# Mixer phase: scans that begin at zero, the old state added to the first column, a third state added by VectorE in four blocks

## The chip, the cores and the metric

One core of one Trainium2 chip runs the whole kernel in one launch. The metric is the time of that core in microseconds (us). Before the change the median of three runs is 5242.94 us (5242.02 to 5242.97). About 0.2% (10 us) is what such a measurement can tell from no change.

## The reference

The input is a tensor of 4 sequences x 2048 tokens x 512 channels in float32. Three layers follow one another: an RWKV-like channel mix (`f1`), a Mamba mixer, and the channel mix again (`f2`). The change is in the mixer alone:

```
h   = layernorm(x); x_in = h - mean(h)
xz  = x_in @ W_in                        # 512 -> 2 x 1024: u's input and the gate z
u   = silu(conv4(xz_first) + conv_b)
B,C = split(u @ W_x)                     # 16 states each
delta = softplus(u @ W_dt + b_dt)
for t:  h = exp(delta_t * A) * h + delta_t * B_t * u_t      # 1024 channels x 16 states
        y_t = sum over states of h * C_t
out = (y + u * D) * silu(z) @ W_out + residual
```

## The kernel before

The mixer goes through the tokens in 32 chunks of T = 256, 8 chunks (MC) to a sequence. In a chunk the 1024 channels are 8 blocks b of 128 partitions, and the 16 states of a block are 4 groups g of SG = 4 states. A (block, group) pair is a unit n = 4b + g, so a chunk has NU = 32 units; g is called the place of a unit in its block below. Each engine has its own instruction list with one slot for each unit, written out by hand. Tables such as `DU_AT`, `DT_AT` and `YG_AT` say in which slot a piece of other work (the convolution, the projections, softplus) stands, and `due(...)` finds what falls into a slot. Semaphores order the engines.

For a unit:

- ScalarE (L1153) writes exp(delta * A) for 4 states into PSUM, two states (`SD`) to a bank, three banks in turn. The half of a unit that goes to bank p may be written when bank p - 3 has been used: for the second half of unit n that is when VectorE's product `times_c` (L1253) of unit n - 1 has been done. `keep_psum` (L1094) and `keep` (L1076) copy the last column of every scan to `hst`, the state carried to the next chunk.
- GpSimd (POOL) makes `mx_dbu` = B * (delta * u) (`times_b`, L947) for two units in one instruction, 128 x 2048 elements, into one of two pairs of buffers; it starts only when the unit three before its first has been scanned. It also makes delta * u (`delta_u`, L964), adds the softplus parts (`add_log`, L935) and multiplies the two SBUF states of a unit by C (`times_c`, L960, mostly two units in one instruction). All of these read and write SBUF.
- VectorE (DVE) runs the four scans of 256 steps (L1241). Each reads the decay from PSUM, dbu from SBUF, and as its initial value a column of `hst` (zero in a sequence's first chunk). Two scans write back to PSUM and are multiplied by C by L1253, two write to `hp` in SBUF.
- TensorE (PE) sums the 16 products of a block into `ps_y` by multiplying with an identity matrix. The last SBUF state of the units at places 2 and 3 is left out there, and VectorE adds it (`add_state`, L1220) before the product with the gate (`gated`, L1227).

At place 0 VectorE also does three convolution taps (L1210). At place 1 it does the two adds and the gated product of the block before last. After the slot of place 1 in every second (odd) block ScalarE switches its function table, does two silu instructions, and switches back (L1182 to L1187).

Of VectorE's instructions in the mixer before the change, none has two tensor inputs in SBUF: scans, L1253, L1210, L1220 and L1227 all read one of their two tensors from PSUM. The channel-mix phases have such instructions, for example L511, L482 and L445.

Of the kernel before, what the change touches and what calls it, by code (L numbers as in the profile page):

```python
# [19 lines left out]
P = 128  # L20
# [667 lines left out]
def mixer_phase(nc, hT_pad, xs_in, ahead, w_dt, w_out, w_k, mu_r, mu_k, bc_dram, out):  # L688
# [8 lines left out]
    with ExitStack() as ctx:  # L697
# [20 lines left out]
        cs = sb("cs", [P, NG, SG, T])  # L718
        bc = sb("bc", [2 * DS, T])
        dbu = sb("dbu", [P, NM, SG, T])  # L720
# [56 lines left out]
        IN_AT = [NG * b - NU - 9 for b in range(ND)]  # L777
        GATE_AT = [NG * b - 11 for b in range(ND)]
        BC_AT, CLEAR = [-10], -1
        DU_AT = [NG * b - 1 for b in range(ND)]  # L780
        DT_AT = [NG * b - 8 for b in range(ND)]
        U_SILU_AT = [2 * NG * k - NU - 3 for k in range(ND // 2)]
        Z_SILU_AT = [2 * NG * k - 3 for k in range(ND // 2)]
        SKIP_AT = [NG * b + NG - 1 for b in range(ND)]
        YG_AT = [NG * b + NG + 5 for b in range(ND)]
        OUT_AT = [NU - 6, NU - 2, NU + 2, NU + 7, NU + 11, NU + 14, NU + 15, NU + 18]
# [38 lines left out]
        def over_chunks(eng, prologue, body, epilogue=None):  # L825

            if prologue:
                prologue()
            for c in range(MC):
                body(c, c % 2, c == 0)  # L830
            with eng.Fori(1, BATCH - 1) as b:
                for c in range(MC):
                    body(MC * b + c, c % 2, c == 0)
            for c in range(MC):
                body(MC * (BATCH - 1) + c, c % 2, c == 0)
            if epilogue:
                epilogue()

        @block.sync
        def _(sp):  # L840
# [8 lines left out]

            def store_bc(i):  # L850

                sp.wait_ge(s_bc, 16 * (i + 1))
                sp.dma_start(bc_dram[:, :], bc[:, :]).then_inc(s_bcd, 16)

# [5 lines left out]
            def chunk(i, par, b_next, c_next):  # L860

                sp.wait_ge(s_pz, ND * (i + 1))
                if not (isinstance(i, int) and i + 2 > LAST):
                    load_hT(b_next, c_next, par)
                if not is0(i):
                    store_out(i - 1)
                    sp.wait_ge(s_out, 16 * i)
                    sp.dma_start(xo[:, :, :], xs_v[i]).then_inc(s_x, 16)
                store_bc(i + 1)
# [15 lines left out]
            sp.dma_start(xo[:, :, :], xs_v[0]).then_inc(s_x, 16)  # L885
            store_bc(0)
            sp.wait_ge(s_bcd, 16)
# [37 lines left out]
        def _(pool):  # L925
# [46 lines left out]

            def body(i, par, first):
# [20 lines left out]
        def _(act):  # L994
# [54 lines left out]

            def copy_bc(c):  # L1050
                act.wait_ge(s_pb, c + 1)
                if not is0(c):
                    act.wait_ge(s_bcd, 16 * c)
                A.activation(bc[:, :], ps_c[0:2 * DS, 0:T], ACT.Copy).then_inc(s_bc, 16)

# [46 lines left out]
            def prologue():  # L1102
                act.wait_ge(s_wv, 16 * 6)
                A.preload_act_table_set("silu_and_others")
                for n in range(EARLIEST, 0):
                    for b, c in due_before(BC_AT, n + 1, COPY):
                        copy_bc(c)
                    for b, c in due_before(IN_AT, n, TAPS):
# [28 lines left out]

            def body(i, par, first):
                for n in range(NU):
# [30 lines left out]
                    for bb, s in due(BC_AT, n, i, COPY):  # L1170
                        copy_bc(i + s)
                    for j, s in due(EVAC_AT, n, i):
# [24 lines left out]
        def _(dve):  # L1197
# [5 lines left out]
            def conv(c, cp, b, step):  # L1203
# [4 lines left out]
                else:  # L1208
                    dve.wait_ge(s_cv, (KC - 2) * ND * c + ((KC - 2) * b + step - 1))
                V.scalar_tensor_tensor(out=q, in0=in_bank(b)[:, step:step + T], scalar=cw[:, step, b:b + 1],  # L1210
                                       in1=q, op0=ALU.mult, op1=ALU.add).then_inc(s_cq if step == KC - 1 else s_cv, 1)

            def add_state(c, b, k):

# [3 lines left out]
                else:  # L1218
                    dve.wait_ge(s_ya, 2 * (ND * c + b) + k)
                V.tensor_tensor(y, y, hp[:, (NG * (b + 1) - 2 + k) % NH, SG - SD - 1, :], ALU.add).then_inc(s_ya, 1)  # L1220

            def gated(c, cp, b):

                q = gy[:, cp, b, :]
                dve.wait_ge(s_zs, ND * c + (b + 1))
                dve.wait_ge(s_ya, 2 * (ND * c + b) + 2)
                V.tensor_tensor(q, y_sum(b), q, ALU.mult).then_inc(s_g, 1)  # L1227
# [5 lines left out]

            def scan(i, n, half, k, first):
                b, g = divmod(n, NG)
                p = 2 * n + half
                if k == 0:
# [18 lines left out]
            def prologue():  # L1256
                weights()
                for n in range(EARLIEST, 0):
                    for b, c in due_before(IN_AT, n, TAPS):
                        for step in range(1, KC):  # L1260
                            conv(c, c, b, step)

            def add_due(i, n, k):

                for b, s in due(YG_AT, n, i):
                    add_state(i + s, b, k)

# [9 lines left out]

            def body(i, par, first):
                for n in range(NU):
                    if not first:  # L1280
                        dve.wait_ge(s_st, NU * i + (n + 1 - NU))
                        if n == 0:
                            dve.wait_ge(s_kd, NU * i - 2)
                        if n == NU - 2:
                            dve.wait_ge(s_kd, NU * i)
# [3 lines left out]
                    scan(i, n, 0, 0, first)  # L1289
                    scan(i, n, 0, 1, first)  # L1290
                    add_due(i, n, 0)
                    scan(i, n, 1, 0, first)
                    taps(i, par, n, 1)
                    times_c(i, n)
                    add_due(i, n, 1)
                    taps(i, par, n, 2)
                    scan(i, n, 1, 1, first)
                    finish(i, par, n)
                    taps(i, par, n, 3)

            def epilogue():
                for n in range(NU):
                    for b in due_after(YG_AT, n):
                        add_state(LAST, b, 0)
                        add_state(LAST, b, 1)
                        gated(LAST, LAST % 2, b)
# [6 lines left out]
        def _(pe):  # L1313
# [228 lines left out]
```

## Time and profile before

| | us |
|---|---|
| median of three runs | 5242.94 |
| the profiled execution itself | 5241.57 |
| its span (first to last instruction) | 5239.8 |
| first to last scan | 709 to 4622 |
| busy: PE / DVE / ACT / POOL | 5133.1 / 4689.6 / 3829.7 / 4029.3 |
| granted TensorE clock, mean | 0.995 of full |

Busy time counts the stretches in which an engine has an instruction under way. Durations of successive instructions on one engine overlap by some tens of ns, so the distance from start to start, called the pitch here, is what a row of instructions costs. The mixer is about 3913 us of the span; its 32 chunks repeat nearly exactly.

### The profile page before, as it was taken

To read this page: it belongs to the slowest core of one execution; us is meant where nothing else is said; L and a number is where in the kernel's file an instruction comes from. 1 tells how busy PE (TensorE), PEld (TensorE's weight loads), DVE (VectorE), ACT (ScalarE), POOL (GpSimd) and SP (SyncE) were. 2 spreads that over 40 slices of the span, in tenths; PEclk is the share of its full clock that TensorE was granted. 3 is DMA by queue.
4 is the path that set the end of the run, shared out by engine and by line. 5 is a ranking of instruction groups with operands and counts; after the bars stand their busy time and mean duration, and the time that the engine had idled before them with its cause. 6 is when DMAs were issued, how large, how long until landed. Compare 5 with 4: busy or idle time off the path is not lost. (4 is left out here: it accounts for less than half of the span.)

```text
span 5239.8 us, 76968 instructions
## 1 busy us (share of the span) xinstructions
PE 5133.1 (98%) x22400; PEld 4127.8 (79%) x22400; DVE 4689.6 (89%) x8052; ACT 3829.7 (73%) x9592; POOL 4029.3 (77%) x1701
## 2 busy tenths in 40 slices
PE   8999989999999999999999999999999999989999
PEld 6777767888888887878888888888888888768887
DVE  7777679999999999999999999999999999977775
ACT  5566568888888888888888888888888888744443
POOL 1111069999999999999999999999999999941110
PEclk9999999999999999999999999999999999989999
DMA  2322231111111111111111111111111111111111
GB/s 83 97 73 86 95 109 45 46 45 53 57 53 49 45 45 46 45 45 45 50 53 47 46 51 56 53 54 45 45 45 45 45 45 45 65 53 57 65 57 41
DMA packets 137371, 291.74 MB, mean 56 GB/s; under 512 B 23280, under 2 KB 40688, under 8 KB 136944
## 3 DMA queue, kind: packets, MB, share of 16 engines
q1 hardware_dynamic: 136944, 286.75, 16.6%
q8 instruction: 183, 3.00, 0.2%
q14 instruction: 244, 2.00, 0.1%
HBM read 218.53 MB, written 68.18 MB: 55 GB/s over the span
## 5 line engine op out<-in xcount | busy, mean ns | idle before, releaser
L947 POOL TENSOR_TENSOR mx_dbu<-mx_bs,mx_du 128x2048 f32<-128x2048 f32 (+1 forms) x513 | 2321.6, 4526 | 64.1 <-POOL mx_du L964 30.5
L1153 ACT ACTIVATE mx_ps_da<-mx_dl,mx_a 128x256 f32<-128x256 f32 x4096 | 1775.9, 465 | 53.8 <-DVE mx_hp L1241 19.0
L1241 DVE TENSOR_TENSOR_SCAN mx_hp<-mx_ps_da,mx_hst,mx_dbu 128x256 f32<-128x256 f32 x1792 | 1317.5, 735 | 31.2 <-ACT mx_ps_da L1153 31.1
L1241 DVE TENSOR_TENSOR_SCAN mx_ps_da<-mx_ps_da,mx_hst,mx_dbu 128x256 f32<-128x256 f32 x1792 | 1238.8, 736 | 62.9 <-ACT mx_ps_da L1153 56.2
L960 POOL TENSOR_TENSOR mx_hp<-mx_hp,mx_cs 128x1024 f32<-128x1024 f32 (+1 forms) x576 | 1219.6, 2123 | 2.1 <-ACT mx_hst L1076 2.1
L1389 PE MATMUL mx_ps_y<-mx_hc,mx_ident 128*128 128x256 f32 x4096 | 1055.4, 380 | 2.5 <-ACT mx_ps_y L1015 2.5
L1356 PE MATMUL mx_ps_m<-mx_u,mx_w_dt 128*128 128x256 f32 x4096 | 926.0, 379 | 1.7 <-issue 1.7
L1389 PEld LDWEIGHTS mx_ps_y<-mx_hc,mx_ident 128*128 128x128 f32 x4096 | 780.4, 191 | 110.7 <-ACT mx_ps_y L1015 3.5
L1399 PE MATMUL mx_ps_y<-mx_hp,mx_ident 128*128 128x256 f32 x3072 | 841.2, 383 | 23.4 <-POOL mx_hp L960 22.3
L1356 PEld LDWEIGHTS mx_ps_m<-mx_u,mx_w_dt 128*128 128x128 f32 x4096 | 778.1, 190 | 108.2 <-issue 2.5
L1399 PEld LDWEIGHTS mx_ps_y<-mx_hp,mx_ident 128*128 128x128 f32 x3072 | 576.5, 190 | 203.3 <-issue 88.5
L1253 DVE TENSOR_TENSOR mx_hc<-mx_ps_da,mx_cs 128x512 f32<-128x512 f32 x1024 | 684.4, 668 | 1.6 <-PE mx_ps_y L1389 1.6
L1094 ACT ACTIVATE mx_hst<-mx_ps_da 128x2 f32<-128x2 f32 x1022 | 171.0, 167 | 599.2 <-DVE mx_hc L1253 596.6
L246 POOL TENSOR_TENSOR f_rstd<-f_ve,f_half 128x4 f32<-128x4 f32 x48 | 48.4, 1008 | 681.6 <-DVE f_ve L413 681.6
L1338 PE MATMUL mx_ps_m<-mx_hT,mx_w_in 128*128 128x256 f32 x2048 | 493.1, 383 | 19.2 <-DVE mx_u L1210 19.0
L1327 PE MATMUL mx_ps_m<-mx_hT,mx_w_in 128*128 128x259 f32 x2048 | 492.8, 383 | 5.1 <-PEq L59 3.2
L1327 PEld LDWEIGHTS mx_ps_m<-mx_hT,mx_w_in 128*128 128x128 f32 x2048 | 389.9, 191 | 104.9 <-issue 46.4
L1366 PE MATMUL mx_ps_c<-mx_w_out,mx_gy 128*128 128x512 f32 x992 | 466.1, 592 | 0.0
L1338 PEld LDWEIGHTS mx_ps_m<-mx_hT,mx_w_in 128*128 128x128 f32 x2048 | 382.3, 190 | 93.8 <-DVE mx_u L1210 42.6
L1210 DVE SCALAR_TENSOR_TENSOR mx_u<-mx_ps_m,mx_cw,mx_u 128x256 f32<-128x256 f32 x768 | 356.4, 464 | 28.6 <-ACT mx_u L1002 27.8
L252 POOL TENSOR_TENSOR mx_w_in<-f_xhT 128x2048 f32<-128x2048 f32 x30 | 111.1, 3703 | 322.0 <-ACT f_xhT L302 322.0
L1366 PEld LDWEIGHTS mx_ps_c<-mx_w_out,mx_gy 128*128 128x128 f32 x992 | 188.5, 190 | 131.4 <-issue 118.6
(122 smaller groups left out, 7323.7 us busy)
## 6 DMA issues: line engine op xcount, KB each, us to landing
mx_bs<-bc_scratch SPq DMA_DIRECT2D x128, 512.0 KB, 4.4
mx_cs<-bc_scratch SPq DMA_DIRECT2D x128, 512.0 KB, 3.8
mx_hT<-hT_scratch SPq DMA_DIRECT2D x32, 518.0 KB, 4.2
hT_scratch<-f_h2T SPq DMA_DIRECT2D x16, 1024.0 KB, 9.1
mx_xo<-xs_scratch SPq DMA_DIRECT2D x32, 512.0 KB, 3.6
x_scratch<-mx_xo SPq DMA_DIRECT2D x32, 512.0 KB, 2.8
f_x<-in_L_attn_inp SPq DMA_DIRECT2D x12, 1024.0 KB, 6.6
xs_scratch<-f_x SPq DMA_DIRECT2D x12, 1024.0 KB, 4.3
```

Source lines behind the costliest of these rows:

```text
L947: G.tensor_tensor(dbu[:, n % NM:n % NM + k].rearrange("p n s t -> p (n s) t"), bs[:, g:g + k].rearrange("p n s t -> p (n s) t"), bcast(du[ ...
L960: G.tensor_tensor(h, h, cs[:, g:g + k, SD:SG, :], ALU.mult).then_inc(s_pr, k)
L1153: ins = A.activation(ps_da[DA_BANK[p]][:, k, :], dl[:, b % NL, :], ACT.Exp, scale=a_sb[:, b, s:s + 1])
L1210: V.scalar_tensor_tensor(out=q, in0=in_bank(b)[:, step:step + T], scalar=cw[:, step, b:b + 1], in1=q, op0=ALU.mult, op1=ALU.add).then_inc( ...
L1241: ins = V.tensor_tensor_scan(da if half == 0 else hp[:, n % NH, k, :], da, dbu[:, n % NM, s, :], 0.0 if first else hst[:, b, SG * g + s:SG ...
L1253: V.tensor_tensor(hc[:, n % NC, :, :], ps_da[DA_BANK[2 * n]][:, :, :], cs[:, g, 0:SD, :], ALU.mult).then_inc(s_m2, 1)
L1327: ins = M.matmul(in_bank(b)[:, 0:TH], w_in_sb[:, f, b * P:(b + 1) * P], hT[cp][:, f, :], start=(f == 0), stop=(f == NB - 1))
L1338: ins = M.matmul(m_bank(b)[:, 0:T], w_in_sb[:, f, DI + b * P:DI + (b + 1) * P], hT[cp][:, f, PAD_L:PAD_L + T], start=(f == 0), stop=(f == ...
L1356: ins = M.matmul(m_bank(b)[:, 0:T], w_dt_sb[:, k, b * P:(b + 1) * P], u[:, cp, k, :], start=(k == 0), stop=(k == ND - 1))
L1366: ins = M.matmul(ps_c[:, :], gy[:, cp, b, j * P:(j + 1) * P], w_out_sb[:, b, :], start=False, stop=(b == ND - 1), skip_group_check=True)
L1389: ins = M.matmul(y_sum(b), ident[:, :], hc[:, n % NC, k, :], start=False, stop=False, skip_group_check=True)
L1399: ins = M.matmul(y_sum(b), ident[:, :], hp[:, n % NH, k, :], start=False, stop=(g == NG - 1), skip_group_check=True)
```

## The change

All scans start from 0.0. What the initial value did is done ahead of the scan: ScalarE computes the decay of a block's first column for all 16 states (`first_decay`), VectorE multiplies the block's 16 kept states by it (`decay_old`; a memset in the very first chunk), and adds the result to the first column of dbu of two units (`add_old`, 128 x 8 elements), except in a sequence's first chunk. The tile `bc` is dropped; its 32 x 256 values pass through the last block of `gy`. In odd blocks VectorE adds a third state, and PE sums one fewer. `delta_u` moves one slot up, to stand ahead of POOL's product with C and no longer directly ahead of the `times_b` that reads it.

```diff
-        bc = sb("bc", [2 * DS, T])
+        e0 = sb("e0", [P, 2, DS])
...
+        E0_AT = [NG * b - 1 for b in range(ND)]
-        DU_AT = [NG * b - 1 for b in range(ND)]
+        DU_AT = [NG * b - 2 for b in range(ND)]
+        ADDED = [[n for n in range(NG * b + 1 + (b % 2 == 0), NG * (b + 1))] for b in range(ND)]
...
+        def bc(cp):
+            return gy[0:2 * DS, cp, ND - 1, :]
...                                     # POOL, body
+                    for bb, s in due(DU_AT, n, i):
+                        delta_u(i + s, (par + s) % 2, bb)
                     for m, s in due(TIMES_AT, n, i):
                         times_c(i + s, TIMES[m])
-                    for bb, s in due(DU_AT, n, i):
-                        delta_u(i + s, (par + s) % 2, bb)
...                                     # ACT
+                if b == ND - 1:                       # in copy_z
+                    act.wait_ge(s_bcd, 16 * (c + 1))
-                if not is0(c):                        # in copy_bc
-                    act.wait_ge(s_bcd, 16 * c)
+                if not (isinstance(c, int) and c < 2):
+                    act.wait_ge(s_po, TJ * (c - 1))
+            def first_decay(c, b):
+                act.wait_ge(s_dl, ND * c + (b + 1))
+                A.activation(e0[:, b % 2, :], a_sb[:, b, :], ACT.Exp, scale=dl[:, b % NL, 0:1]).then_inc(s_e0, 1)
...                                     # ACT, body, at the end of the slot, after log:
+                    for bb, s in due(E0_AT, n, i):
+                        first_decay(i + s, bb)
...                                     # DVE
-                                           0.0 if first else hst[:, b, SG * g + s:SG * g + s + 1], ALU.mult, ALU.add)
+                                           0.0, ALU.mult, ALU.add)
+            def decay_old(i, b):
+                dve.wait_ge(s_e0, ND * i + (b + 1))
+                h = hst[:, b, :]
+                if is0(i):
+                    V.memset(h, 0.0).then_inc(s_hw, 1)
+                    return
+                dve.wait_ge(s_st, NU * (i - 1) + NG * (b + 1))
+                dve.wait_ge(s_kd, NU * (i - 1) + NG * (b + 1))
+                V.tensor_tensor(h, h, e0[:, b % 2, :], ALU.mult).then_inc(s_hw, 1)
+            def add_old(i, n):
+                b, g = divmod(n, NG)
+                dve.wait_ge(s_hw, ND * i + (b + 1))
+                dve.wait_ge(s_m1, NU * i + (n + 2))
+                d = dbu[:, n % NM:n % NM + 2, :, 0]
+                V.tensor_tensor(d, d, hst[:, b, SG * g:SG * (g + 2)].rearrange("p (n s) -> p n s", n=2),
+                                ALU.add).then_inc(s_hb, 1)
...                                     # DVE, body
-                    if not first:
-                        dve.wait_ge(s_st, NU * i + (n + 1 - NU))
...
+                    if c > 0 and n % 2 == 0:
+                        dve.wait_ge(s_hb, NU // 2 * ((MC - 1) * q + (c - 1)) + (n // 2 + 1))
...
-                    scan(i, n, 0, 1, first)
                     add_due(i, n, 0)
+                    if n % NG == NG - 1 and n < NU - 1:
+                        decay_old(i, n // NG + 1)
+                    elif n == NU - 1 and not (isinstance(i, int) and i == LAST):
+                        decay_old(i + 1, 0)
+                    scan(i, n, 0, 1)
+                    add_due(i, n, 1)
+                    scan(i, n, 1, 0)
                     taps(i, par, n, 1)
                     times_c(i, n)
-                    add_due(i, n, 1)
+                    add_due(i, n, 2)
                     taps(i, par, n, 2)
-                    scan(i, n, 1, 1, first)
+                    if n % 2 and n < NU - 1 and c > 0:
+                        add_old(i, n + 1)
+                    elif n == NU - 1 and c < MC - 1:
+                        add_old(i + 1, 0)
+                    scan(i, n, 1, 1)
...                                     # PE, sum_states
-                last = 1 if g >= NG - 2 else 0
+                last = 1 if n in ADDED[b] else 0
```

## Rows read from the trace of the kernel before

**Rows 1.** Windows: us, then busy us of PE, PEld, DVE, ACT, POOL; clock, DMA.
```profile
1565.00:1687.30 122.30, 121.73 (x529) 98.20 (x528) 119.17 (x209) 99.70 (x270) 120.30 (x50) 1.00 0.15 48
1687.30:1808.80 121.50, 121.09 (x527) 97.91 (x526) 112.58 (x209) 99.11 (x270) 119.65 (x51) 1.00 0.15 49
```
**Rows 2.** All scans by line, until 4622 us: ns min/median/max, first and last start.
```profile
L1241 DVE TENSOR_TENSOR_SCAN mx_ps_da<-mx_ps_da,mx_hst,mx_dbu x1792: 720/733/760, 829.2 to 4620.0; 128x256 f32<-128x256 f32 x200
L1241 DVE TENSOR_TENSOR_SCAN mx_hp<-mx_ps_da,mx_hst,mx_dbu x1792: 711/739/752, 830.5 to 4621.8; 128x256 f32<-128x256 f32 x200
L1241 DVE TENSOR_TENSOR_SCAN mx_ps_da<-mx_ps_da,mx_dbu x256: 669/673/699, 709.3 to 3766.9; 128x256 f32<-128x256 f32 x128
L1241 DVE TENSOR_TENSOR_SCAN mx_hp<-mx_ps_da,mx_dbu x256: 660/679/692, 710.8 to 3768.7; 128x256 f32<-128x256 f32 x128
```
**Rows 3.** Timeline of DVE, first scans of chunks 8 and 9: start us, us.
```profile
1687.29 1.25 DVE L1241 TENSOR_TENSOR_SCAN mx_ps_da<-mx_ps_da,mx_dbu 128x256 f32<-128x256 f32 x2
...
1808.81 1.37 DVE L1241 TENSOR_TENSOR_SCAN mx_ps_da<-mx_ps_da,mx_hst,mx_dbu 128x256 f32<-128x256 f32 x2
```
**Rows 4.** Timeline of DVE, first scans of seven units (places 2, 2, 3, 0, 1, 2, 3).
```profile
2047.50 1.40 DVE L1241 TENSOR_TENSOR_SCAN mx_ps_da<-mx_ps_da,mx_hst,mx_dbu 128x256 f32<-128x256 f32 x2 [0.39 <-ACT mx_ps_da L1153]
...
2062.78 1.39 DVE L1241 TENSOR_TENSOR_SCAN mx_ps_da<-mx_ps_da,mx_hst,mx_dbu 128x256 f32<-128x256 f32 x2
...
2065.96 1.38 DVE L1241 TENSOR_TENSOR_SCAN mx_ps_da<-mx_ps_da,mx_hst,mx_dbu 128x256 f32<-128x256 f32 x2
...
2069.13 1.38 DVE L1241 TENSOR_TENSOR_SCAN mx_ps_da<-mx_ps_da,mx_hst,mx_dbu 128x256 f32<-128x256 f32 x2
...
2073.45 1.39 DVE L1241 TENSOR_TENSOR_SCAN mx_ps_da<-mx_ps_da,mx_hst,mx_dbu 128x256 f32<-128x256 f32 x2
...
2078.08 1.40 DVE L1241 TENSOR_TENSOR_SCAN mx_ps_da<-mx_ps_da,mx_hst,mx_dbu 128x256 f32<-128x256 f32 x2 [0.39 <-ACT mx_ps_da L1153]
...
2081.71 1.37 DVE L1241 TENSOR_TENSOR_SCAN mx_ps_da<-mx_ps_da,mx_hst,mx_dbu 128x256 f32<-128x256 f32 x2
```
**Rows 5.** Timeline of ACT in the same stretch.
```profile
2065.42 0.17 ACT L1094 ACTIVATE mx_hst<-mx_ps_da 128x2 f32<-128x2 f32 x1 [0.88 <-DVE mx_hc L1253]
...
2066.54 0.40 ACT L1070 ACTIVATE mx_en<-mx_en 128x256 f32<-128x256 f32 x1
...
2073.41 1.28 ACT L1182 ACT_TABLE_LOAD   x1
...
2077.17 0.87 ACT L1153 ACTIVATE mx_ps_da<-mx_dl,mx_a 128x256 f32<-128x256 f32 x2
...
2082.66 0.40 ACT L1070 ACTIVATE mx_en<-mx_en 128x256 f32<-128x256 f32 x1
```
**Rows 6.** The page's fifth part, the exponentials' row: count, busy, mean ns of one.
```profile
L1153 ACT ACTIVATE mx_ps_da<-mx_dl,mx_a 128x256 f32<-128x256 f32 x4096 | 1775.9, 465 | 53.8 <-DVE mx_hp L1241 19.0
```
**Rows 7.** Timeline of POOL in the same stretch.
```profile
2062.99 4.52 POOL L947 TENSOR_TENSOR mx_dbu<-mx_bs,mx_du 128x2048 f32<-128x2048 f32 x1 [0.22 <-POOL mx_du L964]
2067.48 2.35 POOL L960 TENSOR_TENSOR mx_hp<-mx_hp,mx_cs 128x1024 f32<-128x1024 f32 x1
2069.79 0.72 POOL L935 TENSOR_TENSOR mx_dl<-mx_dl,mx_en 128x256 f32<-128x256 f32 x1
```
**Rows 8.** Timeline of DVE and of POOL about 113 us, in the first phase.
```profile
113.02 3.69 DVE L511 SCALAR_TENSOR_TENSOR f_x<-f_rt,f_x 128x512 f32<-128x512 f32 x1
...
112.56 3.60 POOL L252 TENSOR_TENSOR mx_w_in<-f_xhT 128x2048 f32<-128x2048 f32 x1 [9.11 <-ACT f_xhT L302]
```
**Rows 9.** Lines 511, 508 and 482: ns min/median/max of the whole run.
```profile
L511 DVE SCALAR_TENSOR_TENSOR f_x<-f_rt,f_x x96: 691/693/4120, 113.0 to 5236.6; 128x512 f32<-128x512 f32 x96
L508 DVE SCALAR_TENSOR_TENSOR f_rt<-f_rt,f_ps_v x128: 669/679/690, 73.1 to 5235.9; 128x512 f32<-128x512 f32 x128
L482 DVE SCALAR_TENSOR_TENSOR mx_w_in<-mx_w_in,f_mu,f_xhT x4: 740/1474/1522, 18.5 to 22.7; 128x512 f32<-128x512 f32 x4
```
**Rows 10.** Groups of DVE: the cheapest small instruction in the trace.
```profile
L409 DVE MEMSET f_mark<- 128x1 f32 x48 | 2.8, 59 | 0.0
```

More of the change, by code:

```diff
@@ L755, in mixer_phase @@
         s_da = sem("da_ready")
+        s_e0 = sem("first_decay_ready")
+        s_hw = sem("old_states_decayed")
+        s_hb = sem("old_states_added")
         s_sc = sem("scanned")
@@ L829, in over_chunks @@
             for c in range(MC):
-                body(c, c % 2, c == 0)
+                body(c, c % 2, 0, c)
             with eng.Fori(1, BATCH - 1) as b:
                 for c in range(MC):
-                    body(MC * b + c, c % 2, c == 0)
+                    body(MC * b + c, c % 2, b, c)
             for c in range(MC):
-                body(MC * (BATCH - 1) + c, c % 2, c == 0)
+                body(MC * (BATCH - 1) + c, c % 2, BATCH - 1, c)
             if epilogue:
@@ L848, in spread, with store_bc @@
                              rows.unsqueeze(0).to_broadcast([P, SG * T])).then_inc(done[g], 16)
-            def store_bc(i):
+            def store_bc(i, par):
                 sp.wait_ge(s_bc, 16 * (i + 1))
-                sp.dma_start(bc_dram[:, :], bc[:, :]).then_inc(s_bcd, 16)
+                sp.dma_start(bc_dram[:, :], bc(par)).then_inc(s_bcd, 16)
             def store_out(i):
@@ L868, in chunk @@
                     sp.dma_start(xo[:, :, :], xs_v[i]).then_inc(s_x, 16)
-                store_bc(i + 1)
+                store_bc(i + 1, 1 - par)
                 sp.wait_ge(s_bcd, 16 * (i + 2))
@@ L885, in _ @@
             sp.dma_start(xo[:, :, :], xs_v[0]).then_inc(s_x, 16)
-            store_bc(0)
+            store_bc(0, 0)
             sp.wait_ge(s_bcd, 16)
@@ L971, in prologue, with body @@
                         delta_u(c, c, b)
-            def body(i, par, first):
+            def body(i, par, q, c):
                 for n in range(NU):
@@ L1048, in clear_bc, with copy_bc @@
                              scale=0.0).then_inc(s_bz, 1)
-            def copy_bc(c):
+            def copy_bc(c, cp):
                 act.wait_ge(s_pb, c + 1)
-                if not is0(c):
-                    act.wait_ge(s_bcd, 16 * c)
-                A.activation(bc[:, :], ps_c[0:2 * DS, 0:T], ACT.Copy).then_inc(s_bc, 16)
+                if not (isinstance(c, int) and c < 2):
+                    act.wait_ge(s_po, TJ * (c - 1))
+                A.activation(bc(cp), ps_c[0:2 * DS, 0:T], ACT.Copy).then_inc(s_bc, 16)
             def relu(c, b):
@@ L1106, in prologue @@
                     for b, c in due_before(BC_AT, n + 1, COPY):
-                        copy_bc(c)
+                        copy_bc(c, c)
                     for b, c in due_before(IN_AT, n, TAPS):
@@ L1128, in prologue @@
                             log(c, b)
+                    for b, c in due_before(E0_AT, n):
+                        first_decay(c, b)
                     if due_before(Z_SILU_AT, n):
@@ L1136, in prologue, with body @@
                         A.preload_act_table_set("natural_log_exp_and_others")
-            def body(i, par, first):
+            def body(i, par, q, c):
                 for n in range(NU):
@@ L1170, in body @@
                     for bb, s in due(BC_AT, n, i, COPY):
-                        copy_bc(i + s)
+                        copy_bc(i + s, (par + s) % 2)
                     for j, s in due(EVAC_AT, n, i):
@@ L1211, in conv, with added_before @@
                                        in1=q, op0=ALU.mult, op1=ALU.add).then_inc(s_cq if step == KC - 1 else s_cv, 1)
+            def added_before(c, b):
+                return sum(len(a) for a in ADDED) * c + sum(len(a) for a in ADDED[:b])
             def add_state(c, b, k):
@@ L1218, in add_state @@
                 else:
-                    dve.wait_ge(s_ya, 2 * (ND * c + b) + k)
-                V.tensor_tensor(y, y, hp[:, (NG * (b + 1) - 2 + k) % NH, SG - SD - 1, :], ALU.add).then_inc(s_ya, 1)
+                    dve.wait_ge(s_ya, added_before(c, b) + k)
+                V.tensor_tensor(y, y, hp[:, ADDED[b][k] % NH, SG - SD - 1, :], ALU.add).then_inc(s_ya, 1)
             def gated(c, cp, b):
@@ L1225, in gated @@
                 dve.wait_ge(s_zs, ND * c + (b + 1))
-                dve.wait_ge(s_ya, 2 * (ND * c + b) + 2)
+                dve.wait_ge(s_ya, added_before(c, b + 1))
                 V.tensor_tensor(q, y_sum(b), q, ALU.mult).then_inc(s_g, 1)
@@ L1232, in last_residual, with scan @@
                 V.tensor_tensor(xo[:, j, :], ps_m[j][:, :], xo[:, j, :], ALU.add).then_inc(s_o, 1)
-            def scan(i, n, half, k, first):
+            def scan(i, n, half, k):
                 b, g = divmod(n, NG)
@@ L1261, in prologue @@
                             conv(c, c, b, step)
+                decay_old(0, 0)
             def add_due(i, n, k):
                 for b, s in due(YG_AT, n, i):
-                    add_state(i + s, b, k)
+                    if k + len(ADDED[b]) >= 3:
+                        add_state(i + s, b, k + len(ADDED[b]) - 3)
             def finish(i, par, n):
@@ L1276, in taps, with body @@
                     conv(i + s, (par + s) % 2, b, step)
-            def body(i, par, first):
+            def body(i, par, q, c):
                 for n in range(NU):
-                    if not first:
-                        dve.wait_ge(s_st, NU * i + (n + 1 - NU))
[L1282 to L1285, printed above, removed]
+                    if c > 0 and n % 2 == 0:
+                        dve.wait_ge(s_hb, NU // 2 * ((MC - 1) * q + (c - 1)) + (n // 2 + 1))
                     dve.wait_ge(s_m1, NU * i + (n + 1))
@@ L1288, in body @@
                         dve.wait_ge(s_r, NU * i + (n - NH + 1))
-                    scan(i, n, 0, 0, first)
-                    scan(i, n, 0, 1, first)
+                    scan(i, n, 0, 0)
                     add_due(i, n, 0)
-                    scan(i, n, 1, 0, first)
+                    if n % NG == NG - 1 and n < NU - 1:
[5 more added lines that the diff above has]
+                    scan(i, n, 1, 0)
                     taps(i, par, n, 1)
                     times_c(i, n)
-                    add_due(i, n, 1)
+                    add_due(i, n, 2)
                     taps(i, par, n, 2)
-                    scan(i, n, 1, 1, first)
+                    if n % 2 and n < NU - 1 and c > 0:
[3 more added lines that the diff above has]
+                    scan(i, n, 1, 1)
                     finish(i, par, n)
@@ L1303, in epilogue @@
                     for b in due_after(YG_AT, n):
-                        add_state(LAST, b, 0)
-                        add_state(LAST, b, 1)
+                        for k in range(len(ADDED[b])):
+                            add_state(LAST, b, k)
                         gated(LAST, LAST % 2, b)
@@ L1419, in prologue, with body @@
                 pe.wait_ge(s_wo, 16)
-            def body(i, par, first):
+            def body(i, par, q, c):
                 for n in range(NU):
```

## The prediction

> **What bounds the kernel now.** I read the windows first [rows 1], because the change is in the mixer only. In an ordinary chunk of 122.3 us PE is busy 121.7, POOL 120.3 and DVE 119.2: three engines within 2%, so busy shares can't name the bound. The reader should instead look at what repeats. The first scan that takes an old state starts at 829.20 [rows 2], the next sequence's first scan at 1687.29 [rows 3]: 7 chunks, 122.58 us each. A sequence's first chunk, whose scans begin at zero already, takes 1808.81 - 1687.29 = 121.52 [rows 3]. There DVE is busy 6.6 us less [rows 1], yet the chunk is only 1.1 shorter: POOL and PE stand right behind.
>
> The timeline of DVE shows the loop. From one unit after a silu to the next is 2078.08 - 2047.50 = 30.58 us [rows 4]; four such pairs of blocks are 122.3. Units take 3.18 (place 2), 3.17 (3), 4.32 (0) and, without the 0.39 idle and 0.08 of pipeline tail at its end, 4.16 (1): 14.83 a block [rows 4]. Two blocks are 29.66; the other 0.9 is DVE waiting for ScalarE's exponentials behind the silu: 0.47 before place 2, and as much inside it (3.63 against 3.18). ScalarE in turn waits for DVE's product, since its banks come free by it (0.88 idle in one place [rows 5]). POOL shows 0.22 idle in each block, behind its own `delta_u` [rows 7]. So DVE with ScalarE is the bound, by tenths of a us.
>
> **The change part by part.**
>
> *Scans from zero.* 733 becomes 673 ns and 739 becomes 679 [rows 2]: 0.06 less. 128 scans are 7.7 us in each of 28 chunks; in 4 chunks nothing. Per block: 14.83 - 0.96 = 13.87.
>
> *Third added state.* An add has a pitch of about 0.33 (256 columns; a product of 512 takes 0.58 from start to start, as unit lengths give). In odd blocks, one more: +0.33, and PE loses two records of about 0.22 each in such a block, 1.7 us a chunk, on an engine with little idle. It falls at place 1 of the odd blocks, where DVE waits 0.47 for the silu anyway, so I cost most of it at nothing there.
>
> *`delta_u` sooner.* It takes away POOL's 0.22 in each of 8 blocks [rows 7], 1.8 us a chunk of an engine that would become the bound next. Its waiters, the pair product two instructions later, see nothing else. `add_log` and the SP queue stay as they are; the `bc` rows sit in `gy` long after the output product has read it, and the new wait in `copy_z` comes some 26 slots behind the store. Nothing.
>
> *`first_decay`.* 8 on ScalarE in a chunk. Nearest rows: 0.17 us for 2 columns [rows 5], 0.465 for 256 [rows 6]; I take 0.25, bounds 0.17 and 0.465. ScalarE has 22 us of room a chunk; what counts is when it is ready. It stands at the end of the slot of place 3, behind `log`. `log` starts 0.58 after the unit's first scan (2066.54 against 2065.96), after a silu 0.95 (2082.66 against 2081.71) [rows 4, 5], and has a pitch of 0.3. Ready: 1.17 and 1.54 after the unit starts. `decay_old` is reached after one scan, at 0.59, and behind it in DVE's in-order queue are all further scans. Alone this costs 0.6 and about 1.0, and 0.1 more in each as the scans of DVE shorten.
>
> *The two-SBUF-input additions.* `decay_old` (8 a chunk) and `add_old` (16) are the first DVE instructions of the mixer whose two tensors both lie in SBUF, and they run beside POOL instructions of up to 4.52 us [rows 7]. How this goes is shown in the first phase: L511, two SBUF tensors, started at 113.02, while POOL's product ran from 112.56 to 116.16, and took 3.69 us, to 116.71; its median is 0.69 [rows 8, 9]. L508, the same size but with one tensor in PSUM, never took more than 0.69 in the run [rows 9]. With POOL instructions back to back, L482 took 1.47 to 1.52 instead of 0.74 [rows 9]: it waits for the one under way and gets its turn before the next. So each of the 24 waits for the end of the POOL instruction under way. The instruction itself I take at 0.07, from the memset's 0.059 [rows 10]; upper bound 0.2 (a 512-column product's 0.67 less its columns at about 1 ns).
>
> The Trainium skill, page "SBUF — State Buffer", section "SBUF: two separate sides", says that a VectorE instruction with two SBUF inputs and a GpSimd one share a pair of ports as an exclusive lock for the whole instruction. The rows agree for 512 columns; that it holds for 8 columns of a tensor_tensor too only the page says, no row here.
>
> Now the walk through a block without silu; 0 is the start of place 0.
> - POOL, released by the unit before, makes a pair product 0.17 to 4.66, `delta_u` to 5.37, the states' product to 7.68 (pitches 4.49, 0.7, 2.31 [rows 7]).
> - DVE: place 0 lasts 4.08; in place 1 it reaches `add_old` at 7.06, waits to 7.68 (0.62), and starts place 2 at 8.69. POOL starts the next pair product at 8.55 (it waited for this unit), to 13.04.
> - DVE: place 2 lasts 2.93; at 12.21 it reaches `decay_old`, waits to 13.04 (0.83; the e0 wait lies inside it), goes on at 13.14. POOL's states' product runs 13.11 to 15.42.
> - DVE reaches `add_old` at 14.9, waits to 15.42 (0.52), ends the block at 16.12.
>
> With a silu (odd block): `add_old` in place 1 waits 0.3 because the third add took the rest; place 2 starts at 8.83 and has 0.55 idle inside; `decay_old` is reached at 12.9, but e0 is ready only at 14.0 (8.83 + 2082.66 - 2078.08 + 0.3 + 0.25). POOL has taken the port at 13.05 for 2.31, so it waits to 15.4: 2.5 us. The later `add_old` finds POOL idle. Block: 17.88. The pair is 34.0, a chunk 136.0; at the chunk's ends POOL's products are single (half as long), which I estimate to shorten two waits by 0.6: 134.8. Against 122.58: +12.2.
>
> In a sequence's first chunk there is no `add_old`: 34.0 less its waits (0.62, 0.52, 0.3) and 4 x 0.07 is 32.3, 129.1 a chunk, +7.6.
>
> Sum: 28 x 12.2 + 4 x 7.6 = 372. On the profiled execution, 5241.6 (span 5239.8 and 1.8 around it, 1.4 under the median of three), that is 5613; the first chunk partly fills only, so I say 5610. PE, with 1.7 us less work in a 12 us longer chunk, and POOL wait for DVE then.
>
> **The rivals.**
>
> *A. The lock holds (above).* For: rows 8 and 9. Against: those instructions have 512 columns. Bounds: with 0.03 for a small instruction -25 us, with 0.2 +100; if arrivals fall luckier, half the port waits: 5480. Own range 5450 to 5720.
>
> *B. No lock for such small instructions; the e0 wait remains.* Pair: 29.66 - 1.92 + 0.33 + 6 x 0.07 = 28.5, idle behind the silu 0.1 and 0.55, e0 waits 0.65 and 1.1: 30.9 to 31.2, against 30.58. A chunk is 124.6, +2.1, the four first ones +2: 5310. The range is 5280 to 5340.
>
> *C. Faster.* POOL's port is free when DVE needs it and ScalarE runs ahead enough that e0 is there: then DVE (28.5 and 0.65 idle for a pair, 116.6) is below POOL, whose 122.3 lose 8 x 0.22. Chunk 120.5; 28 x -2.1 and 4 x -1 give 5180. For: POOL and PE show that room [rows 1]. Against: `log`'s place in rows 5. It decides only if both waits are under 0.2 us each.
>
> *D. Both signs cancel* within 0.2%: small waits of 0.3 eat the gain of C: 5242.
>
> **How the numbers follow.** A 0.68, B 0.13, C 0.13, D 0.06. Predicted is A's time. Slower (over 0.2%, about what this measurement can tell) is A and B, 0.81; same 0.06; faster 0.13. The range must leave out no more than 2 in 10: 5300 to 5720 holds A and half of B.
>
> **What would show it.** In the trace after: `decay_old` and `add_old` rows of 0.06 to 3 us, with ends shortly after the end of a POOL row; scans all at 0.68; POOL idle before L947, released by DVE's scans; DVE idle at place 3 before `decay_old`, released by ScalarE; PE with visible waits. If those small rows all last under 0.2 us A is wrong; if DVE isn't idle before `decay_old` in every block, B too; if the POOL's pair products follow without idle, it is C.

## The result and the profile after

The changed kernel takes 5581.19 us (median of 4 runs, 5579.58 to 5583.03), the kernel before 5242.48 on the same chip: 1.0644 times as long, 95% interval 1.063 to 1.0657. The forecast was 5610. The profiled execution took 5583.03, its span is 5581.2 against 5239.8.

The page's first part of the kernel after (busy us, share of the span, instructions), and from its fifth part three groups (count, busy us, mean ns of one, idle us before them and what ended it):
```profile
PE 5176.2 (93%) x22144; PEld 4104.9 (74%) x22144; DVE 4878.1 (87%) x8884; ACT 3885.8 (70%) x9848; POOL 4036.5 (72%) x1701
...
L956 POOL TENSOR_TENSOR mx_dbu<-mx_bs,mx_du 128x2048 f32<-128x2048 f32 (+1 forms) x513 | 2318.8, 4520 | 394.0 <-DVE mx_hp L1263 383.0
...
L1387 PE MATMUL mx_ps_m<-mx_hT,mx_w_in 128*128 128x256 f32 x2048 | 547.3, 413 | 304.2 <-DVE mx_u L1229 303.9
...
L1277 DVE TENSOR_TENSOR mx_hst<-mx_hst,mx_e 128x16 f32<-128x16 f32 x248 | 189.9, 766 | 200.3 <-ACT mx_e L1081 200.3
```
POOL's pair product (L947 before, L956 now) stands idle 394 us, nearly all of it for DVE's scans; PE waits 304 us for DVE's taps. Both were close behind DVE before; now they wait for it. `decay_old` (L1277) shows two costs in one row: 200.3 us idle before it, ended by ScalarE's `first_decay` (L1081), and 766 ns for an instruction of 16 columns. Before the change the scans' lines had 75.9 and 48.4 us idle for ScalarE's exponentials; these are now:
```profile
DVE mx_hp L1263 <- ACT mx_ps_da L1170: 48.9, 123, 0.4
...
DVE mx_ps_da L1263 <- ACT mx_ps_da L1170: 20.7, 45, 3.1
```
That is a view of waits: us in total, times, the longest. DVE's account closes: busy 188.5 us more (4878.1 against 4689.6), idle for e0 200.3 more, idle for exponentials 54.7 less: 334 of the 341.4 us by which the span grew. TensorE's mean granted clock is 0.984 of full here and was 0.995 before, but no term of this account is a wait for PE, and PE is the one that waits.

An ordinary chunk and a sequence's first chunk, as windows, beside [rows 1] (us; busy us of PE, PEld, DVE, ACT, POOL; clock, DMA share, GB/s):
```profile
2437.50:2571.10 133.60, 123.30 (x522) 97.62 (x521) 125.05 (x238) 101.63 (x279) 120.78 (x51) 0.99 0.13 44
3896.50:4025.40 128.90, 122.51 (x522) 96.65 (x521) 119.07 (x221) 101.51 (x281) 120.69 (x52) 1.00 0.14 46
```
133.6 where 134.8 was forecast, and 128.9 where it was 129.1. POOL's busy time in a chunk is what it was (120.8, before 120.3), in 11 us more of chunk.

The timeline of DVE over two blocks, without and with a silu (start us, length us, idle before and its releaser):
```profile
2469.41 1.25 DVE L1263 TENSOR_TENSOR_SCAN mx_ps_da<-mx_ps_da,mx_dbu 128x256 f32<-128x256 f32 x2
...
2476.50 0.68 DVE L1285 TENSOR_TENSOR mx_dbu<-mx_dbu,mx_hst 128x8 f32<-128x8 f32 x1
2477.09 0.68 DVE L1263 TENSOR_TENSOR_SCAN mx_hp<-mx_ps_da,mx_dbu 128x256 f32<-128x256 f32 x1
...
2480.95 0.67 DVE L1263 TENSOR_TENSOR_SCAN mx_ps_da<-mx_ps_da,mx_dbu 128x256 f32<-128x256 f32 x1
2482.20 0.28 DVE L1277 TENSOR_TENSOR mx_hst<-mx_hst,mx_e 128x16 f32<-128x16 f32 x1 [0.59 <-ACT mx_e L1081]
2482.40 0.68 DVE L1263 TENSOR_TENSOR_SCAN mx_ps_da<-mx_ps_da,mx_dbu 128x256 f32<-128x256 f32 x1
...
2484.17 0.63 DVE L1285 TENSOR_TENSOR mx_dbu<-mx_dbu,mx_hst 128x8 f32<-128x8 f32 x1
2484.72 0.68 DVE L1263 TENSOR_TENSOR_SCAN mx_hp<-mx_ps_da,mx_dbu 128x256 f32<-128x256 f32 x1
2485.31 1.25 DVE L1263 TENSOR_TENSOR_SCAN mx_ps_da<-mx_ps_da,mx_dbu 128x256 f32<-128x256 f32 x2
...
2492.73 0.37 DVE L1285 TENSOR_TENSOR mx_dbu<-mx_dbu,mx_hst 128x8 f32<-128x8 f32 x1
2493.02 0.68 DVE L1263 TENSOR_TENSOR_SCAN mx_hp<-mx_ps_da,mx_dbu 128x256 f32<-128x256 f32 x1
...
2497.54 0.67 DVE L1263 TENSOR_TENSOR_SCAN mx_ps_da<-mx_ps_da,mx_dbu 128x256 f32<-128x256 f32 x1
2499.25 1.47 DVE L1277 TENSOR_TENSOR mx_hst<-mx_hst,mx_e 128x16 f32<-128x16 f32 x1 [1.04 <-ACT mx_e L1081]
2500.64 0.68 DVE L1263 TENSOR_TENSOR_SCAN mx_ps_da<-mx_ps_da,mx_dbu 128x256 f32<-128x256 f32 x1
```
And POOL's instructions that these meet:
```profile
2474.78 2.37 POOL L969 TENSOR_TENSOR mx_hp<-mx_hp,mx_cs 128x1024 f32<-128x1024 f32 x1
2477.91 4.53 POOL L956 TENSOR_TENSOR mx_dbu<-mx_bs,mx_du 128x2048 f32<-128x2048 f32 x1 [0.77 <-DVE mx_hp L1263]
2482.41 2.36 POOL L969 TENSOR_TENSOR mx_hp<-mx_hp,mx_cs 128x1024 f32<-128x1024 f32 x1
...
2498.32 2.35 POOL L969 TENSOR_TENSOR mx_hp<-mx_hp,mx_cs 128x1024 f32<-128x1024 f32 x1
```
The ends are what to read. The add at 2476.50 ends at 2477.18, POOL's states' product at 2477.15. The `decay_old` at 2482.20 ends at 2482.48, the pair product at 2482.44. The add at 2484.17 ends at 2484.80, the product at 2484.77. The `decay_old` at 2499.25 ends at 2500.72, the product at 2500.67. Each of these small instructions is over 0.03 to 0.05 us behind a POOL row, however early it began. The whole trace says the same: 241 of the 248 `decay_old` rows and 338 of the 448 `add_old` rows last over 0.2 us, and every one of these ends 0.03 to 0.04 us after the end of a POOL row. DVE is counted as busy while it waits so: no view of waits names it.

### The profile page after: what moved, and what is told of

Its sections match the earlier page's. It is cut to its first block and busy times, and to the rows that moved or that the text cites. A ratio compares the mean times of both kernels' runs of the same rounds, so it can differ in the third digit from the quotient of the medians.

```text
span 5581.2 us, 77770 instructions
## 1 busy us (share of the span) xinstructions
PE 5176.2 (93%) x22144; PEld 4104.9 (74%) x22144; DVE 4878.1 (87%) x8884; ACT 3885.8 (70%) x9848; POOL 4036.5 (72%) x1701
## 5 line engine op out<-in xcount | busy, mean ns | idle before, releaser
L956 POOL TENSOR_TENSOR mx_dbu<-mx_bs,mx_du 128x2048 f32<-128x2048 f32 (+1 forms) x513 | 2318.8, 4520 | 394.0 <-DVE mx_hp L1263 383.0
L1263 DVE TENSOR_TENSOR_SCAN mx_hp<-mx_ps_da,mx_dbu 128x256 f32<-128x256 f32 x2048 | 1371.4, 670 | 49.0 <-ACT mx_ps_da L1170 48.9
L1263 DVE TENSOR_TENSOR_SCAN mx_ps_da<-mx_ps_da,mx_dbu 128x256 f32<-128x256 f32 x2048 | 1325.9, 674 | 31.6 <-ACT mx_ps_da L1170 20.7
L1438 PEld LDWEIGHTS mx_ps_y<-mx_hc,mx_ident 128*128 128x128 f32 x4096 | 787.3, 192 | 120.3 <-ACT mx_ps_y L1024 9.7
L1387 PE MATMUL mx_ps_m<-mx_hT,mx_w_in 128*128 128x256 f32 x2048 | 547.3, 413 | 304.2 <-DVE mx_u L1229 303.9
L1448 PE MATMUL mx_ps_y<-mx_hp,mx_ident 128*128 128x256 f32 x2816 | 793.7, 386 | 29.5 <-POOL mx_hp L969 29.4
L1448 PEld LDWEIGHTS mx_ps_y<-mx_hp,mx_ident 128*128 128x128 f32 x2816 | 535.8, 192 | 203.6 <-issue 81.7
L246 POOL TENSOR_TENSOR f_rstd<-f_ve,f_half 128x4 f32<-128x4 f32 x48 | 48.4, 1008 | 681.1 <-DVE f_ve L413 681.1
L1277 DVE TENSOR_TENSOR mx_hst<-mx_hst,mx_e 128x16 f32<-128x16 f32 x248 | 189.9, 766 | 200.3 <-ACT mx_e L1081 200.3
```

The source lines that it names most:

```text
L956: G.tensor_tensor(dbu[:, n % NM:n % NM + k].rearrange("p n s t -> p (n s) t"), bs[:, g:g + k].rearrange("p n s t -> p (n s) t"), bcast(du[ ...
L1387: ins = M.matmul(m_bank(b)[:, 0:T], w_in_sb[:, f, DI + b * P:DI + (b + 1) * P], hT[cp][:, f, PAD_L:PAD_L + T], start=(f == 0), stop=(f == ...
L1438: ins = M.matmul(y_sum(b), ident[:, :], hc[:, n % NC, k, :], start=False, stop=False, skip_group_check=True)
L1448: ins = M.matmul(y_sum(b), ident[:, :], hp[:, n % NH, k, :], start=False, stop=(g == NG - 1), skip_group_check=True)
```

## The experiments

Ratios are against the kernel before, whose medians in these comparisons were 5243.7 to 5244.8 us. "The lock" stands for the wait of a DVE instruction with two tensors in SBUF for the POOL instruction under way.

**e1_one_sbuf_input.** The kernel after; the second tensor of both small instructions comes from a PSUM bank. Count, shapes, places and semaphores stay; the old states are then not those that the reference asks for.
```diff
-                V.tensor_tensor(h, h, e0[:, b % 2, :], ALU.mult)
+                V.tensor_tensor(h, h, ps_da[DA_BANK[(2*NG*b - 1) % (2*NU)]][:, 1, 0:DS], ALU.mult)
-                V.tensor_tensor(d, d, hst[:, b, SG*g:SG*(g+2)]..., ALU.add)
+                V.tensor_tensor(d, d, ps_da[DA_BANK[(2*n - 1) % (2*NU)]][:, 1, 0:2*SG]..., ALU.add)
```


> The kernel after, with the same 24 small VectorE instructions in a chunk, the same waits and the same order, but the second tensor of each is read from a PSUM bank that VectorE holds at that moment instead of from SBUF (so the values of the old states are not those of the reference). Lock theory: no small row waits for a GpSimd instruction, each has a pitch of about 0.1 us and a duration under 0.3; the wait of decay_old for the first decay stays (about 0.65 us in even and 1.1 in odd blocks); a chunk is 124 to 125 us instead of 133.7, the whole 5300 to 5325. Rival, that small instructions or the e0 wait are dear in themselves: over 5500, unchanged.

5327.45 us, ratio 1.016 (1.0139 to 1.018). By line (ns min/median/max, first and last start), first of after, then of this kernel:
```profile
L1277 DVE TENSOR_TENSOR mx_hst<-mx_hst,mx_e x248: 174/316/3203, 831.1 to 4944.5; 128x16 f32<-128x16 f32 x124
L1285 DVE TENSOR_TENSOR mx_dbu<-mx_dbu,mx_hst x448: 153/376/1870, 833.0 to 4954.1; 128x8 f32<-128x8 f32 x150
```
```profile
L1277 DVE TENSOR_TENSOR mx_hst<-mx_hst,mx_ps_da x248: 170/171/173, 834.3 to 4692.5; 128x16 f32<-128x16 f32 x124
L1285 DVE TENSOR_TENSOR mx_dbu<-mx_dbu,mx_ps_da x448: 154/158/173, 836.1 to 4702.0; 128x8 f32<-128x8 f32 x150
```
None of the 696 rows lasts over 173 ns any more, and 254 of the 339 us are gone. The time is 2 us above the range that was expected. What remains, 83 us over before, is B's mechanism: `decay_old` still stands idle for e0.
```profile
DVE mx_hst L1277 <- ACT mx_e L1081: 200.9, 248, 1.2
```

**e2_decay_sooner.** The kernel after; `first_decay` one unit sooner, the lock left in.
```diff
-        E0_AT = [NG * b - 1 for b in range(ND)]
+        E0_AT = [NG * b - 2 for b in range(ND)]
```


> The kernel after with first_decay one slot sooner on ScalarE (at the end of place 2 instead of place 3), nothing else. Theory: the 200 us of idle before decay_old go, but in even blocks the wait for the GpSimd instruction takes its place, and in odd blocks decay_old now meets the end of the pair product instead of missing it, about 2.3 us sooner, of which later port waits take back half; a chunk is 129 to 131 us, the whole 5440 to 5500. If the e0 wait were independent of the port, all of its 200 us would come off: 5380.

5453.39 us, 1.04 (1.0379 to 1.0421). The idle time before `decay_old` is gone, but the same instructions meet POOL sooner in its product and last longer; the groups of DVE (busy us, mean ns, idle us):
```profile
L1277 DVE TENSOR_TENSOR mx_hst<-mx_hst,mx_e 128x16 f32<-128x16 f32 x248 | 252.1, 1016 | 0.0
L1285 DVE TENSOR_TENSOR mx_dbu<-mx_dbu,mx_hst 128x8 f32<-128x8 f32 x448 | 247.3, 552 | 0.0
```
Of 200 us idle, 128 were gained. The rows of `decay_old` grew by 62 us (766 to 1016 ns, 248 times) and those of `add_old` by 40; by DVE's busy time, which counts overlaps once (4960.9 against 4878.1), 83 us came back.

**e3_both.** Both edits, with `decay_old` one scan later and, for the bank that it reads, one wait more. As in e1 the second tensors come from PSUM.
```diff
+                    scan(i, n, 0, 1)
                     if n % NG == NG - 1 and n < NU - 1:
                         decay_old(i, n // NG + 1)
...
-                    scan(i, n, 0, 1)
```


> Both edits together: second tensors from PSUM and first_decay one slot sooner; decay_old stands one scan later, where the bank it reads is ready anyway (old states not those of the reference). Theory: both waits are gone, VectorE needs about 117 us a chunk, and GpSimd (120.3 busy) or PE is the bound: chunk 120.5 to 121.5, whole 5175 to 5215, faster than the kernel before. Rival (ScalarE's banks bound the loop anyway): 5240 or more.

5207.35 us, 0.9931 (0.9911 to 0.9951): below before. A stretch of 600 us in the middle:
```profile
2100.00:2700.00 600.00, 593.73 (x2572) 479.73 (x2571) 573.33 (x1161) 496.33 (x1374) 594.21 (x248) 1.00 0.15 50
```
DVE is busy 573 of 600, PE and POOL 594 each. The rest of the change is worth 36 us once both waits are out of the way: rival C's gain exists, and PE and POOL have no room left there, as C said. Its sum was 5180. DVE's own idle time in the scans of e3 was still for ScalarE's exponentials (151 us), so what of the three holds the last part wasn't separated.

**e7_only_decay_locked, e8_only_add_locked.** The kernel after with one of e1's two edits each: in e7 only `decay_old` has two tensors in SBUF, in e8 only `add_old`.

> The kernel after with the second tensor of add_old (16 a chunk) from PSUM; decay_old keeps its two SBUF tensors (old states not those of the reference). Lock theory, walked through by the trace's pitches: a chunk 128 to 129.5, whole 5410 to 5450. If add_old carried all of the loss: 5330.

> The kernel after with the second tensor of decay_old (8 a chunk) from PSUM; add_old keeps its two SBUF tensors. Lock theory: a chunk 128.5 to 130, a sequence's first chunk 124 to 125, whole 5420 to 5460. The two gains of 130 to 160 us are more than the 254 us that both together gave, since each wait shifts the other's arrival.

e7: 5478.15 us, 1.0446 (1.0425 to 1.0467), 28 us above the expected range; why the walk came out too low for it stays open. e8: 5459.12, 1.041 (1.0389 to 1.043), as expected. The claim that the two gains taken singly exceed the joint one fell: 103 + 122 = 225, jointly 254. The groups of e7, then of e8:
```profile
L1277 DVE TENSOR_TENSOR mx_hst<-mx_hst,mx_e 128x16 f32<-128x16 f32 x248 | 194.9, 786 | 201.1 <-ACT mx_e L1081 201.1
L1285 DVE TENSOR_TENSOR mx_dbu<-mx_dbu,mx_ps_da 128x8 f32<-128x8 f32 x448 | 69.3, 155 | 0.0
```
```profile
L1285 DVE TENSOR_TENSOR mx_dbu<-mx_dbu,mx_hst 128x8 f32<-128x8 f32 x448 | 234.2, 523 | 0.0
L1277 DVE TENSOR_TENSOR mx_hst<-mx_hst,mx_ps_da 128x16 f32<-128x16 f32 x248 | 42.6, 172 | 200.5 <-ACT mx_e L1081 200.5
```
Locked, less free, times the count, is what each waits: e7 (786 - 171) x 248 = 152.5 us, and the kernel is 150.7 longer than e1. e8 (523 - 158) x 448 = 163.5, and it is 131.7 longer. `decay_old`'s waits are paid in full, four fifths of `add_old`'s. Locking both costs less than the two alone (254 against 151 + 132). The rows show where the 29 us go. In the kernel after, `add_old` is
```profile
L1285 DVE TENSOR_TENSOR mx_dbu<-mx_dbu,mx_hst 128x8 f32<-128x8 f32 x448 | 206.9, 462 | 0.0
```
462 ns against 523 in e8, 27 us in 448, and `decay_old` 766 against 786 in e7, 5 us in 248: with `decay_old` held up too, `add_old` waits less. That it then arrives nearer to the end of POOL's instruction would explain it; no run shows that alone.

**e5_before_16_sbuf_sbuf, e6_before_16_psum_sbuf.** The kernel before; ahead of the last scan of every odd unit one multiply of 8 columns whose result nothing uses, with both tensors in SBUF (e5) or the second in PSUM (e6).
```diff
+                V.tensor_tensor(dbu[:, n % NM, 0, 0:2*SG], a_sb[:, 0, 0:2*SG], a_sb[:, 1, 0:2*SG], ALU.mult)  # e5
+                V.tensor_tensor(dbu[:, n % NM, 0, 0:2*SG], a_sb[:, 0, 0:2*SG], bank[:, 1, 0:2*SG], ALU.mult)  # e6
```


> The kernel before with one added VectorE multiply of 8 columns before the last scan of every odd unit (16 a chunk), both tensors in SBUF, no wait, its result unused. Lock theory: each waits for the end of the GpSimd instruction under way; by the pitches of the trace before, a chunk grows from 122.6 to about 131 us, the whole to 5480 to 5540. Rival (a small instruction costs its own 0.07 to 0.16 us): 5265 to 5330.

> The same 16 multiplies a chunk, but the second tensor read from PSUM. Lock theory: only their own pitch of about 0.07, some of it in VectorE's idle: 5260 to 5290. If such small instructions were dear by themselves it would be as slow as with both tensors in SBUF.

e5: 5444.42 us, 1.0381 (1.036 to 1.0402), below the expected range. e6: 5266.4, 1.0042 (1.0026 to 1.0058), as expected. Groups of e5, then of e6:
```profile
L1258 DVE TENSOR_TENSOR mx_dbu<-mx_a 128x8 f32<-128x8 f32 x512 | 319.2, 623 | 0.0
```
```profile
L1258 DVE TENSOR_TENSOR mx_dbu<-mx_a,mx_ps_da 128x8 f32<-128x8 f32 x512 | 82.0, 160 | 0.0
```
The two kernels differ in where 8 columns lie, and in 178 us: 0.35 for each of 512. With one tensor in PSUM an instruction costs 23 us / 512 = 0.04. This is the cleanest proof, since nothing waits for these instructions and they wait for no semaphore of their own. The same lines, ns min/median/max and first and last start:
```profile
L1258 DVE TENSOR_TENSOR mx_dbu<-mx_a x512: 151/394/1862, 715.5 to 4823.4; 128x8 f32<-128x8 f32 x171
```
```profile
L1258 DVE TENSOR_TENSOR mx_dbu<-mx_a,mx_ps_da x512: 150/159/183, 720.6 to 4648.6; 128x8 f32<-128x8 f32 x171
```
In e6's trace 484 of the 512 begin and end inside a POOL row, undisturbed. In e5's not one does: 458 last over 0.2 us, and each of these ends 0.02 to 0.03 us after the end of a POOL row. So it is POOL's instruction that they wait for, and the place of the second tensor that makes them wait. The expectation for e5 had 8.4 us a chunk, 0.53 for each; measured are 0.39 in time and a mean wait of 623 - 160 = 463 ns in the rows, with a median of 394 - 159 = 235: most arrive late in POOL's instruction of up to 4.5 us.

**e4_before_du_sooner, e11_before_third.** The change's two other parts, each alone on the kernel before: `delta_u` one unit sooner and ahead of the states' product; the third added state in odd blocks.
```diff
-        DU_AT = [NG * b - 1 for b in range(ND)]
+        DU_AT = [NG * b - 2 for b in range(ND)]   # e4, with the delta_u loop ahead of times_c
+        ADDED = [[n for n in range(NG*b + 1 + (b % 2 == 0), NG*(b + 1))] for b in range(ND)]   # e11
```


> The kernel before with delta_u one slot sooner and ahead of the product with C, nothing else. Theory: GpSimd's 0.22 us of idle in each block goes, but VectorE with ScalarE is the bound (122.55 us a chunk), so the time stays within 0.2%: 5232 to 5248. Rival, that GpSimd is the bound: 1.8 us a chunk less, 5185.

> The kernel before with the third added state in odd blocks alone. Theory: it lies in VectorE's 0.47 us of idle before place 2 behind a silu, and what it takes from PE is not on the path: 5232 to 5250. If PE were the bound, 1.7 us a chunk less: 5190.

5240.58 us, 0.9992 (0.9982 to 1.0002), and 5241.7, 0.9996 (0.9986 to 1.0005), 10 runs each: nothing, as the forecast costed them. In e4 POOL's idle time behind its own `delta_u` (30.5 us before) is gone from the waits, and the one behind DVE's scans rose from 22.0 to 61.8: POOL waits for DVE instead.

**e9_before_relu_later, e10_before_relu_third, e12_after_sooner_relu.** If ScalarE's work behind the silu is what DVE waits for [rows 4], moving its relu pair from behind the first pair of exponentials of a unit to behind the second should take that wait away. e9 is the kernel before with this and e4's edit, e10 is e9 with e11's, e12 is e2 with the relu moved (lock left in).
```diff
-                        if half == 0:
+                        if half == 1:
                             for bb, s in due(DT_AT, n, i, RELU):
                                 relu(i + s, bb)
+                        if half == 0:
                             for bb, s in due(IN_AT, n, i, TAPS):
```


> The kernel before with delta_u one slot sooner and with ScalarE's two softplus reads (Abs and Relu) moved behind the second pair of exponentials of their slot. Theory: the idle of VectorE inside place 2 after a silu (0.45 us, 4 times a chunk) goes, GpSimd has room since delta_u is sooner: chunk 121 to 121.7, whole 5190 to 5220. If VectorE's waits at the silu merely move to its other place: 5235 to 5242.

> The same with the third state added by VectorE in odd blocks, scans unchanged. Theory: the third add lies in the idle before place 2 after a silu and takes 1.7 us a chunk from PE, which is nearly full: 5185 to 5215, at most 10 us below the kernel without it. If VectorE has no idle left there, it costs 4 x 0.33 a chunk: up to 40 us more.

> The kernel after with first_decay a slot sooner and the softplus reads behind the second pair of exponentials. Theory: the port waits stay (24 two-SBUF instructions a chunk), the idle inside place 2 goes, of which the port waits take back a part: chunk 127.5 to 129, whole 5385 to 5440, still slower than before. If the port waits could be scheduled away like this: under 5300.

e9: 5225.12 us, 0.9966 (0.9954 to 0.9979), 5 us above the expected range: in the timeline only the idle time inside place 2 went, the one before its first scan stays.
```profile
2042.82 1.40 DVE L1242 TENSOR_TENSOR_SCAN mx_ps_da<-mx_ps_da,mx_hst,mx_dbu 128x256 f32<-128x256 f32 x2 [0.39 <-ACT mx_ps_da L1153]
```
e10: 5216.5, 0.9946 (0.9929 to 0.9963), 1.5 us above its range. The third add, worth nothing alone, is worth 9 us there; the two intervals overlap, the runs don't (e9 at least 5223.5, e10 at most 5218.0). 550 us of e10:
```profile
2100.00:2650.00 550.00, 545.23 (x2355) 438.33 (x2354) 546.32 (x959) 449.85 (x1225) 544.14 (x227) 1.00 0.15 50
```
PE, DVE and POOL are all busy 99% of it. e10 computes all that the reference asks, and is 27 us faster than the kernel before and 365 than the one after. e12: 5424.25, 1.0343 (1.0322 to 1.0364), within what was expected and 29 us below e2: even with e0 early and the relu moved, the lock keeps the change above before.

## Why the prediction was right

- **The likeliest case was A, and the lock is shown** by e1 and by e5 against e6: it holds for 8 and 16 columns, and for the whole POOL instruction. The Trainium skill, page "SBUF — State Buffer", section "SBUF: two separate sides", says that a VectorE instruction with two SBUF inputs and a GpSimd instruction that reads SBUF exclude each other for the whole of the one that starts first. These runs bear it out, for GpSimd's starting first, at a width that no row of before had.
- **The attribution.** The lock costs 254 us (after less e1). The e0 wait costs 120 without the lock (e1 less e3, whose `decay_old` is also a scan later) and 128 with it (after less e2). The rest of the change gives back 36 (e3 against before). That 254 + 120 - 36 = 338 meets the measured 339 proves nothing by itself, since these are steps through the same kernels. The rows are the independent sign: in the kernel after the two kinds wait (766 - 171) x 248 = 148 us and (462 - 158) x 448 = 136 us, 284 in rows for 254 in time. The forecast had B alone at 5310, so 300 for the lock and 67 for the rest; measured are 254 and 83. The two misses have opposite signs, so part of the total's nearness (29 us) is luck: the lock alone was 46 off.
- **The walk.** DVE's waits in the block without silu were forecast 0.62, 0.83 and 0.52. Measured, from the pitch to the next scan less 0.07 and less the scan ahead of it: 0.52 (2476.50 to 2477.09), 0.78 (2480.95 to 2482.40 less 0.60 and 0.07) and 0.48 (2484.17 to 2484.72). In the block with silu 0.3, 0.55 and 2.5 against 0.22, 0.44 and 2.43 (2497.54 to 2500.64 less 0.60 and 0.07). The even `decay_old` waits 0.59 of its 0.78 for e0 and only the rest for POOL; the walk had said that the e0 wait lies inside. Blocks took 15.90 and 17.76 (2469.41, 2485.31, and 2503.07 for the next) where 16.12 and 17.88 were forecast.
- **The sum.** The walk gave 372, the two spans differ by 341.4. The term that was too large is the ordinary chunk: 28 x (134.8 - 133.6) = 34 us. The waits for POOL above are each 0.04 to 0.1 shorter than forecast. The first chunks were right to 0.2.
- **`first_decay`** was taken at 0.25 and lasts 0.29. The 1.17 and 1.54 us at which the prediction has e0 ready are 0.04 more than its own terms add up to (0.58 or 0.95, 0.3, 0.25); the walk uses the terms and isn't touched. A small two-tensor instruction was taken at 0.07, and 2468.74 to 2468.81 in the timeline of DVE is 0.07.
- **Parts costed at nothing.** `delta_u` and the third add alone are within 0.1% of before (e4, e11). Both were tried on the kernel before; what either is worth inside the kernel after, no run shows.
- **C** was rightly low: its condition (each wait under 0.2 us) had to be built, in e3, by changing the data's place and e0's slot. Its 5180 was 27 us too low, against a bound by PE and POOL that it named.

## What stays open

Whether a version of this change that keeps old states and has no lock exists wasn't tried: the old states would have to lie in PSUM beside the banks of the scans, or POOL itself would have to add them. Why some waits span several POOL instructions (below) is open too, and why e7 was 28 us above its range. Whether a small DVE instruction that comes first holds POOL up in turn, no run here was made to show.

## What to carry to other kernels

Before a small VectorE instruction is added beside a busy GpSimd, ask where its two tensors lie: one of them in PSUM cost 0.04 us here, both in SBUF 0.39, and the trace books the wait as busy time. The price is set by when the instruction arrives in GpSimd's row, so it can be estimated by walking one period with both engines' pitches: within 30 us of 339 here, though the ranges from such a walk were missed by 36 us in e5 and 28 in e7. A value that ScalarE makes for an in-order engine belongs one slot ahead of its use: ready 0.6 to 1.0 us late it cost a third of this loss by itself.

## What the runs showed that I had not expected

A waiting instruction usually gets its turn between two POOL instructions that follow without a gap: that at 2499.25 went on at 2500.64, where POOL's next began. But not always. In e2, DVE and then POOL:
```profile
825.90 6.18 DVE L1277 TENSOR_TENSOR mx_hst<-mx_hst,mx_e 128x16 f32<-128x16 f32 x1
```
```profile
824.38 4.53 POOL L956 TENSOR_TENSOR mx_dbu<-mx_bs,mx_du 128x2048 f32<-128x2048 f32 x1
828.87 2.50 POOL L969 TENSOR_TENSOR mx_hp<-mx_hp,mx_cs 128x512 f32<-128x512 f32 x2
831.32 0.72 POOL L944 TENSOR_TENSOR mx_dl<-mx_dl,mx_en 128x256 f32<-128x256 f32 x1
```
It waited through four POOL instructions, to 832.08, and POOL's last ended at 832.04. This is rare: 4 of the 248 in the kernel after and 12 of the 248 in e2 waited past the end of a first POOL instruction.

An unblocked small instruction lasts 0.15 to 0.17 us in its row but takes 0.07 from start to start, so its row's length says little of its price, and a minimum of the line is needed to read a wait out of a longer one.
